# Three chunks of the down weights are looked up between gate and up tiles, and two units and one slot move in the stages before

## The reference, cut to what matters

```python
x = _layernorm(x + _L0_attn_ref(x, ...))            # first attention, 8 heads, 8 blocks of 128 rows
x = _layernorm(x + _L0_xattn_ref(ctx, ctx, x))      # sims, softmax, context
x = _layernorm(x + _L0_ffn_ref(x, ...))             # W, and a low-rank part whose rank is chosen per row
x = _layernorm(x + _L1_attn_ref(x, codes, scales, lora))
...
def _dequant(codes, scales):
    w = NF4[codes]                                  # 16 values
    return (w.reshape(O, I // 64, 64) * scales[:, :, None]).reshape(O, I)

def _L1_attn_ref(x, ...):
    attn = (q(x) + k(x) + v(x)) / 3.0               # each W and lora, 512 x 512
    x1 = x + o(attn)
    h = silu(gate(x1)) * up(x1)                     # 512 -> 1792
    return x1 + down(h)                             # 1792 -> 512
```

## Time and profile before

| | us |
|---|---|
| median of 3 runs | 638.48 |
| the profiled execution | 638.13 |
| its span, first to last instruction | 636.3 |
| TensorE busy in the span | 623.6 |
| VectorE, ScalarE, GpSimd busy | 439.2, 402.7, 67.5 |
| mean granted TensorE clock | 0.997 of full |

### The profile page before, as it was taken

How to read it: one execution, slowest core, us unless ns; L and a number is a source line. 1 busy time by engine, 2 the same in 40 slices (tenths; PEclk the granted TensorE clock), 3 DMA queues, 4 the chain that set the end, 5 groups by cost and what they waited for, 6 DMA issues and landing times.

```text
span 636.3 us, 8678 instructions
## 1 busy us (share of the span) xinstructions
PE 623.6 (98%) x3186; PEld 461.7 (73%) x3186; DVE 439.2 (69%) x700; ACT 402.7 (63%) x578; POOL 67.5 (11%) x116
## 2 busy tenths in 40 slices
PE   8999999999999999999999999999999999999995
PEld 6655555544558888888888888887777888887874
DVE  4788787768888877777857437325575777777467
ACT  2977798977988597667677136222458545667532
POOL 1032132311240000000000000001221000000012
PEclk9999999999999999999999999999999999999998
DMA  7762486513254133323330003029000133200002
GB/s 249 287 199 103 155 270 199 155 45 122 66 144 124 55 112 112 107 72 112 106 106 1 2 0 134 1 83 410 2 2 33 49 101 99 68 1 1 1 33 100
DMA packets 25592, 63.94 MB, mean 100 GB/s; under 512 B 5541, under 2 KB 10725, under 8 KB 24782
## 3 DMA queue, kind: packets, MB, share of 16 engines
q1 hardware_dynamic: 23294, 61.68, 29.9%
q10 hardware_dynamic: 2256, 1.70, 0.9%
HBM read 58.77 MB, written 4.60 MB: 100 GB/s over the span
## 4 chain that ended last, share of the span: by engine, by line
PE 86%; DVE 4%; ACT 4%; DMA 2%; issue 2%; SPq 1%; POOL 0%; ACTq 0%; POOLq 0%; DVEq 0%
PE bank L1098 19%; PE bank L1234 10%; PE bank L1086 8%; PE bank L1085 8%; PE bank L1087 8%; PE bank L937 4%; PE bank L857 3%; PE bank L661 3%; PE bank L796 2%; PE bank L1176 2%; PE bank L1177 2%; PE bank L1152 1%; DMA codes<-in_c_qkv 1%; PE bank L967 1%; PE bank L981 1%
## 5 line engine op out<-in xcount | busy, mean ns | idle before, releaser
L1370 ACT ACTIVATE line<-line 128x1024 f32<-128x1024 f32 x87 | 91.4, 1050 | 0.2
L1086 PE MATMUL bank<-xl,wh 128*128 128x512 f32 x224 | 87.4, 390 | 0.0
L1085 PE MATMUL bank<-xh,wh 128*128 128x512 f32 x224 | 87.4, 390 | 0.0
L1087 PE MATMUL bank<-xh,wl 128*128 128x512 f32 x224 | 87.3, 390 | 0.0
L1098 PE MATMUL bank<-wh,xh 128*128 128x512 f32 x176 | 69.8, 397 | 0.2 <-DVE xl L2341 0.2
L1098 PE MATMUL bank<-wh,xl 128*128 128x512 f32 x176 | 68.6, 390 | 0.0
L2341 DVE TENSOR_TENSOR xl<-arena,xh 128x1024 fp32r<-128x1024 f32 (+1 forms) x24 | 28.3, 1180 | 35.7 <-ACT xh L1674 35.5
L1674 ACT ACTIVATE xh<-arena 128x1024 fp32r<-128x1024 f32 (+1 forms) x24 | 24.4, 1022 | 39.6 <-PE bank L1098 35.3
L1087 PEld LDWEIGHTS bank<-xh,wl 128*128 128x128 f32 x224 | 42.1, 188 | 8.8
L1085 PEld LDWEIGHTS bank<-xh,wh 128*128 128x128 f32 x224 | 42.1, 188 | 8.6
L1086 PEld LDWEIGHTS bank<-xl,wh 128*128 128x128 f32 x224 | 42.1, 188 | 8.5
(11 more groups left out here) (287 smaller groups left out, 1374.8 us busy)
## 6 DMA issues: line engine op xcount, KB each, us to landing
codes<-in_c_gu SPq DMA_DIRECT2D x14, 512.0 KB, 3.7
scales<-in_s_gu SPq DMA_DIRECT2D x28, 256.0 KB, 3.8
codes<-in_t_gu SPq DMA_DIRECT2D x8, 512.0 KB, 3.6
codes<-in_c_dn SPq DMA_DIRECT2D x7, 512.0 KB, 5.2
scales<-in_s_dn SPq DMA_DIRECT2D x14, 256.0 KB, 4.3
fold<-in_t_dn SPq DMA_DIRECT2D x1, 3584.0 KB, 15.5
codes<-in_c_qkv SPq DMA_DIRECT2D x6, 512.0 KB, 4.4
scales<-in_t_gu SPq DMA_DIRECT2D x6, 512.0 KB, 3.6
```

What stands on the lines that cost most here:

```text
L1085: pe.matmul(dst, wh[:, s, c:c + P], xh[:, k, cols], start=(k == 0), stop=False)
L1086: pe.matmul(dst, wh[:, s, c:c + P], xl[:, k, cols], start=False, stop=False)
L1087: last = pe.matmul(dst, wl[:, s, c:c + P], xh[:, k, cols], start=False, stop=(k == KD - 1))
L1370: nc.scalar.activation(below(slot), below(slot), ACT.Prelu, bias=bias, scale=scale, alpha=alpha).then_inc(bent, 1)
```

## The change

Of the seven down chunks three (`LATE`: 4, 5, 6) leave the stretch of units and get places right behind gate/up chunks 2, 5 and 8 in the ring's order; `at_gu` and `at_dn` give the places. So there are 24 units instead of 30, and `PLAN` gives the first attention 5 instead of 7 (slots 6 and 7 have none), the cross-attention stage 7 instead of 9, the feed-forward stage 10 instead of 12, spread as 2, 2, 1, 1, 1, 1, 1, 1 instead of 2, 1, 1, 2, 2, 2, 1, 1. `attention_lora`, its additions and the matrix products (`FIRST_M`) come one slot later. The rounding copy to `wh` goes from ScalarE (`gu_hi`) to VectorE (`gu_split`). `down_lora` and `fold_add` come one tile later. SyncE's order of loads follows.

```diff
+LATE = {2: 4, 5: 5, 8: 6}
+C_GU = C_DN + NF // 2 - len(LATE)
+C_END = C_DN + NF // 2 + NF
...
-PLAN = ([0] + [1] * (NT - 1), [2], [0, 1, 1, 1, 2] + [1] * 4, [2, 1, 1, 2, 2, 2, 1, 1, 0, 0])
+PLAN = ([0] + [1] * 5, [2], [0] + [1] * 7, [2, 2] + [1] * (NT - 2))
...
+def at_gu(j):
+
+    return C_GU + j + sum(after < j for after in LATE)
...
+def at_dn(n):
+
+    after = [j for j in LATE if LATE[j] == n]
+    return at_gu(after[0]) + 1 if after else C_DN + n
...
-FIRST_M = 3
+FIRST_M = 4
...
             for b in range(2, 4):
                 context_in(b)
-            load_codes(C_O)
             sp.wait_ge(pv_ps, NT)
             context_T(1)
             for b in range(4, NT - 1):
                 context_in(b)
+            load_codes(C_O)
...
+            for c in range(C_GU, C_END):
+                what, n = AT[c]
+                slot = c % RING
+                sp.wait_ge(bent, BENDS * (c - RING) + READS)
+                sp.dma_start(codes[:, slot, :], i["c_" + what][slice(n, n + 1), :, :].rearrange("o p c -> (o p) c")).then_inc(in_gu[slot], 16)
+                if what == "gu":
+                    if n >= 2:
+                        sp.wait_ge(stack_low, 3 + n - 1)
+                    sp.dma_start(b_gu[:, n % 2, :], i["b_gu"][n]).then_inc(in_bgu[n % 2], 16)
+                sp.wait_ge(scaled, c - RING + 1)
...
-                for n in range(AF0 * t, min(AF0 * (t + 1), 2 * KD)):
+                for n in range(AF0 * (t - 1), min(AF0 * t, 2 * KD)) if t else ():
                     attention_lora(n)
...
-                    if j >= 3:
-                        pe.wait_ge(fold_kept, min(2 * (j - 2), NF))
+                    if j >= 4:
+                        pe.wait_ge(fold_kept, min(2 * (j - 3), NF))
...
-                    if tg and 1 <= j <= NF // 2:
+                    if tg and 2 <= j <= NF // 2 + 1:
                         pe.wait_ge(lora_added, j + 2)
-                        for f in range(2 * j - 2, 2 * j):
+                        for f in range(2 * j - 4, 2 * j - 2):
                             down_lora(f)
...
-            def gu_step(s, j, n_after):
+            def gu_step(s, j):
 
                 if j + 2 < NF:
                     b_high(j + 2)
                 for tg in range(TG):
-                    bend_below(C_GU + j + 1, gu_slot(1 - s), 2 + tg)
+                    bend_below(at_gu(j + 1), gu_slot(j + 1), 2 + tg)
                     silu(1 - s, j - 1, tg)
-                if n_after is not None:
-                    gu_first_bends(s, j + 2, n_after, (w_ready, j + 1))
-                act.wait_ge(up_ps, 2 * j + 2)
-                gu_hi(1 - s, j + 1)
+                if j + 1 in LATE:
+                    c = at_dn(LATE[j + 1])
+                    late_first_bends(c)
+                    for n in range(2, LEAD):
+                        bend_below(c, c % RING, n)
+                if j + 2 < NF:
+                    late_first_bends(at_gu(j + 2))
...
+            def gu_split(s, j):
+
+                dve.wait_ge(lora_added, j + 1)
+                if j >= 2:
+                    dve.wait_ge(up_ps, 2 * j)
+                nc.vector.tensor_copy(wh[:, s, :], weight(gu_slot(j))).then_inc(hi_ready, 1)
                 dve.wait_ge(hi_ready, j + 1)
-                nc.vector.tensor_tensor(wl[:, s, :], weight(gu_slot(s)), f32(wh[:, s, :]), ALU.subtract).then_inc(w_ready, 1)
+                nc.vector.tensor_tensor(wl[:, s, :], weight(gu_slot(j)), f32(wh[:, s, :]), ALU.subtract).then_inc(w_ready, 1)
...
+            def gu_weights(s, j):
+
+                gu_to_scale(s, j)
                 gu_lora_add(s, j)
                 hidden(s, j - 2)
-                if more:
+                if j + 1 < NF:
+                    if j not in LATE:
+                        gu_join_above(1 - s, j + 1)
+                    b_lower(j + 1)
+                gu_split(s, j)
+                if j in LATE:
+                    c = at_dn(LATE[j])
+                    join_above(c, c % RING)
+                    join_below(c, c % RING)
+                    scale_chunk(c)
+                for f in range(max(2 * j - 6, 0), min(2 * j - 4, NF)):
+                    fold_add(f)
+                if j in LATE:
                     gu_join_above(1 - s, j + 1)
```

More of the change, by code:

```diff
@@ L107, in plan @@
     return list(range(first, first + PLAN[phase][t]))
+def at_gu(j):
[3 more added lines that the diff above has]
+    return at_gu(after[0]) + 1 if after else C_DN + n
+assert C_GU % RING == 0 and at_gu(NF - 1) == C_END - 1
+AT = {at_gu(j): ("gu", j) for j in range(NF)} | {at_dn(n): ("dn", n) for n in LATE.values()}
 def key_span(t):
@@ L586, in _ @@
             sp.dma_start(bT0[0:RMAX + 1, :], i["bT0"]).then_inc(in_ffn0, 16)
-            load_scales(C_O)
             keys_out(1)
-            load_codes(C_O + 1)
             sp.dma_start(a_down[:, :], i["a_d"]).then_inc(in_lora, 16)
             sp.dma_start(bT_d[0:STACK, :], i["bT_d"]).then_inc(in_lora, 16)
[L592 to L597, removed]
+            keys_out(2)
+            load_codes(C_O + 1)
+            keys_out(3)
+            load_scales(C_O)
+            keys_out(4)
+            load_codes(C_O + 2)
+            keys_out(5)
+            load_scales(C_O + 1)
+            keys_out(6)
+            load_codes(C_O + 3)
+            keys_out(7)
             for g in range(TG):
@@ L601, in _ @@
                 sp.dma_start(beta_dram[c:c + 1, :], beta_s[c * ROWG:c * ROWG + 1, :]).then_inc(kb_out, 16)
-            for c in range(C_O + 1 + NT // 2, C_GU):
+            load_scales(C_O + 2)
+            for c in range(C_O + 4, C_GU):
                 load_codes(c)
[L604 to L618, removed]
-                                     i["s_gu"][slice(j, j + 1), half, :].partition_broadcast(BLOCK).rearrange("p o c -> p (o c)")).then_inc(in_gus[s], 16)
+                load_scales(c - 1)
+            load_scales(C_GU - 1)
+            for c in range(C_GU, C_END):
[8 more added lines that the diff above has]
+                sp.wait_ge(scaled, c - RING + 1)
+                for half in range(2):
+                    sp.dma_start(scales[half * BLOCK:(half + 1) * BLOCK, slot, :],
+                                 i["s_" + what][slice(n, n + 1), half, :].partition_broadcast(BLOCK).rearrange("p o c -> p (o c)")).then_inc(in_gus[slot], 16)
             for n in range(2):
@@ L1392, in early_bends, with weight_free, late_first_bends @@
                     bend_below(c, c % RING, n)
-            def gu_first_bends(s, j, n, free):
-                act.wait_ge(in_gu[s], 16 * (n + 1))
-                bend_first(C_GU + j, gu_slot(s))
-                bend_second(C_GU + j, gu_slot(s), free)
+            def weight_free(c):
+                what, n = AT[c - RING]
+                return (w_ready, n + 1) if what == "gu" else (scaled, c - RING + 1)
+            def late_first_bends(c):
+                gu_codes_landed(act, c)
+                bend_first(c, c % RING)
+                bend_second(c, c % RING, weight_free(c))
             def unit_bends(u, part):
@@ L1967, in scale_chunk @@
                 if c >= C_O:
[L1968 to L1969 removed]
+                    if c < C_GU:
+                        scales_landed(dve, c)
+                    else:
+                        gu_scales_landed(dve, c)
+                    n = c - C_DN if c < C_GU else AT[c][1]
+                    dst = woT[:, 2 * (c - C_O):2 * (c - C_O) + 2, :] if c < C_DN else fold[:, 2 * n:2 * n + 2, :]
                     nc.vector.scalar_tensor_tensor(dst.rearrange("p k c -> p (k c)"), weight(c), NEAR_UP, scales[:, c % RING, :],
@@ L2296, in gu_weights @@
                     gu_join_above(1 - s, j + 1)
-                    b_lower(j + 1)
-                gu_low(s, j)
-                for f in range(2 * j - 4, min(2 * j - 2, NF)):
-                    fold_add(f)
             gu_join_above(0, 0)
```

95 lines of the change are left out of this document (44 added, 51 removed).

## The result

The changed kernel takes 640.04 us (median of 20 runs, 638.38 to 642.18) against 638.39 of the kernel before (20 runs, 636.78 to 640.67): ratio 1.0025, 95% interval 1.0017 to 1.0032, that is 1.1 to 2.0 us slower. Forecast were 639.5 (1.0 slower) and a range of 636.8 to 642.3. The profiled execution took 640.34, its span is 638.4.

The account below looks back on a forecast made before the run. TensorE was taken as the bound, busy 623.6 of 636.3 us. Terms -0.3 - 0.6 - 0.35 - 0.3 + 0.2 + 1.2 + 1.2 = +1.05 gave 639.2, and 639.5 us as median; range 636.8 to 642.3.

Parts of the forecast that it names:

- Relief: Waits gone at 72.74 (-0.3), 109.61 (-0.6), 182.70 (-0.35) and the last x1_T at 215.99 (-0.3).
- the wait at 182.70: Feed-forward slots, x_T waiting for x_low: goes since the slots with two units are gone, -0.35 us.
- the x1 stretch: Before tile 0: copy off ScalarE brings the last x1_T, at 215.99, net 0.3 us earlier.
- ffn_W(4): Slot 2: TensorE waits for ln_head of block 1 behind one more join in slot 1, +1.2 us (0.9 to 1.4).
- It isn't paid back: The +1.2 us wait at ffn_W(4) stays lost, since the products after it are all still to come.
- attention_out(0): Slot 7: waits for m_low_of(3) at the end of a three-turn chain, +1.2 us (0.9 to 2.0).
- The copy: Rounding copy on VectorE takes 0.69 us each; covered between tiles, -0.3 before tile 0.
- The rival of 1.22: Copy on VectorE runs at one element a cycle, 1.22 us: 640.0 us in all; chance 0.06.
- At tiles 5 and 8: nothing: Chunks between tiles cost no time there; lateness hits gu_lora_add and hidden, needed only at the next tile's middle.
- relief wins: Rival: the two new waits, at ffn_W(4) and attention_out(0), don't come; 636.9 us; chance 0.24.
- the stall at tile 2: Rival: b_gu(3) lands after 5.0 us, VectorE too full, two stalls of 1.4; 642.5 us; chance 0.12.
- doesn't do what it says: Rival: ScalarE waits for codes, earlier stages aren't relieved, four waits stay and new ones come; 641.1 us; chance 0.06.

Follow-up runs that it names:

- e10: Changed kernel with the stages before the feed-forward part put back as before the change, no units in feed-forward slots 0 and 1; 639.74 us, ratio 1.0023.
- e1: Changed kernel with one unit moved from slot 1 to slot 4 of the feed-forward stage; 640.19 us, ratio 1.0029.
- e6: Changed kernel with four edits: unit from slot 1 to 4, m_high_of(3) ahead of norm_tail, b_gu ahead of codes, fold_add ahead of down chunk; 636.75 us, ratio 0.9982.
- e2: Changed kernel with ScalarE's m_high_of(3) ahead of norm_tail in slot 7; 638.45 us, ratio 1.0006.
- e7: Changed kernel with VectorE's x_low right behind ln_head in slots 4 and 6, ahead of the slot's scaling; 638.73 us, ratio 1.0005.
- e3: Changed kernel with the load of b_gu ahead of the 512 KB load of codes in SyncE's queue; 638.84 us, ratio 1.0006.
- e5: Changed kernel with VectorE's fold_add ahead of the down chunk's joins and scaling in tiles 5 and 8; 638.79 us, ratio 1.0014.

## Why the prediction was right, and where it wasn't

**Relief** (-0.3 - 0.6 - 0.35 - 0.3 = -1.55). The first two were 1.17 and not 0.9 (e10 gives them back whole); the third, the wait at 182.70, is gone; the x1 stretch gave 0.17 instead of 0.3, and 0.15 of it are the copy's move (e8, with the copy back on ScalarE, has -0.02 there and the last x1_T's bracket again, 0.29). With 0.34 for the third that is -1.68.

**ffn_W(4)** (+1.2). From 144.16, where attention_lora's start and 1.06 put it, to 145.45: 1.29. Its cause, the second join in slot 1, is shown by e1. "It isn't paid back" was wrong by half: e1 shows that alone it isn't a price at all, since the chain to attention_out(0) ends at 187.9 with it and without it. It counts only once the chain is loosened, and then for half (e6).

**attention_out(0)** (+1.2, of 0.9 to 2.0). 0.81 up to its first matmul, and 0.91 from the start of W to the x_T behind it (8.00 against 7.09 before the change); 0.91 is what e2 gave back, to 0.01, so I count that. TensorE came 17.91 behind ln_head of slot 4 (17.9 forecast); the chain needed 18.72 and not 19.95: the turn with x_low behind ln_head saved 1.14 (5.43 instead of 6.57, GpSimd's first operation 0.23 and its third 0.77 instead of 1.03), and I had taken 0.8 of that. The mechanism is shown from two sides, e2 (the end of the chain) and e7 (its links).

**The ports.** In the slots of the feed-forward stage GpSimd's first operation was 1.10 to 1.12 beside an operation with two SBUF inputs and 0.23 beside x_low, which reads PSUM. It is 0.23 beside an idle VectorE too, in the first attention of the changed kernel:

```profile
62.66 0.23 POOL L1938 TENSOR_SCALAR rstd<-mv 128x1 f32<-128x1 f32 x1 [5.55 <-DVE mv L2037]
```

So 0.23 is what it takes when nothing holds it. Held, it ends 0.08 us behind VectorE's operation: in slot 4 the join runs from 170.65 to 171.86 and GpSimd's operation to 171.94. The Trainium skill, page "SBUF — State Buffer", section "SBUF: two separate sides", says that a VectorE operation with two SBUF inputs and a GpSimd operation that reads SBUF lock each other out of a shared pair of ports. The runs agree with that lock. e1 adds what it costs a chain: the three operations took 4.03 us beside two joins and a scaling, and 1.57 in e7.

**The copy** (0.69). It is 0.69:

```profile
213.76 0.69 DVE L2301 CAST wh<-line 128x1024 fp32r<-128x1024 f32 x1
```

The rival of 1.22 falls. The Trainium skill, page "VectorE: DVE Perf Modes", section "The perf-mode tier table", puts an fp32 copy within SBUF at two elements a cycle and an operation of two tensors at one; 0.69 for this rounding copy of 1024 elements, against 1.22 for `gu_lora_add` of as many, agrees.

**The tiles.** At tile 2 there are +0.15 (+0.2 forecast), in tile 9 nothing. The step that failed is "At tiles 5 and 8: nothing". At tile 5 it is +0.72, and 0.06 behind it. I had followed the excess to gu_lora_add and hidden, for which TensorE asks at the tile's middle, and not to fold_add, which the change puts behind the chunk and for which TensorE asks at the tile's start. And I had priced b_gu right behind the codes for tile 2 alone, with a landing of 1.8 to 5.0 whose median speaks for loads issued later. In the kernel before three of the fourteen were issued 0.6 us behind codes, and those took 4.8 to 5.0. In the changed kernel eleven are issued 0.4 to 0.6 us behind codes. All its loads of b_gu:

```profile
DMA to landing us min/median/max: 1.8/4.6/6.8
```

In most tiles the change turned a load issued 1.7 to 2.8 us behind the codes into one issued 0.4 to 0.6 us behind them. e3 and e5 show each of the two as a condition. At tile 8 the same pair leaves no gap: fold_add ends at 311.1 and TensorE comes at 312.18.

**The sum.** Forecast -1.55 + 1.2 + 1.2 + 0.2 = +1.05; measured -1.68 + 1.29 + 0.91 + 0.15 + 0.78 = +1.45 (1.40 by the table), and +1.65 in the medians. That the forecast time was near was in part luck: the 0.3 too much at attention_out(0) and the 0.1 too little relief met a part of the 0.8 missing at the tiles. The range's upper end has a slip: half of a stall of 2.8 is 1.4, not 1.9, and with it the end would have been 641.7; the measured 640.04 lies inside either way. Of the rivals, "relief wins" failed as argued, for both waits came; the stall at tile 2 failed, for ScalarE waited 2.2 us for b_gu(3) and tile 2 lost 0.15, not 2.8; "doesn't do what it says" failed by e10, which gives back the relief of the stages before; the copy at one element a cycle failed by its 0.69.

Open is what sets the head, ahead of the second x_T; nothing was tried there.

## What to carry to other kernels

A wait that goes is worth nothing while a chain that another engine turns ends at the same place; loosen the end of the chain first (one swap in a queue gave 0.9 us of trace here), then a wait ahead of it pays, here for half. When work is put between two steps of a queue, look for what now stands behind it and which start, not only which middle, waits for that; and when a small load is put behind a large one, price it at the large one's landing. Work moved out of a crowded stretch pays only if it is also spread well where it lands: here 1.7 us of relief were outweighed by 3.1 us of new waits, and four edits of order gave back all but 0.7 us of them.

## What the runs showed of the hardware

A 96 KB load that was issued 0.4 to 0.6 us behind one of 512 KB on the same queue landed 3.6 to 6.8 us after its issue (eleven loads of the changed kernel; 4.8 to 5.0 for three of the kernel before). Issued 1.7 to 3.0 us behind the large one it landed in 1.8 to 3.1 (ten loads of the kernel before, two of the changed one). In e3 it goes ahead of the codes. The five loads there with no other load issued in the 2 us before them landed in 1.9, and those issued right behind two 256 KB loads of scales in 3.5 to 5.5, which is why e3's median is still 3.7.

GpSimd's operations on 128x1 are anything from 0.23 to 1.59 us, by what VectorE runs beside them, and the ones behind are pushed from start to start by as much. The order of a slot on VectorE is thus a lever on GpSimd's latency, and no list of waits names the VectorE operation that holds GpSimd.
